# Expert rows of an AdaLN attention + MoE kernel: added onto the output in DRAM by indirect DMAs, in place of a buffer of picks, its loads and the last additions

## The reference

```python
# mod: six rows of 128 per batch from _silu(c) @ wmod; ga, gb with magnitude of at least 0.25
h = _layernorm(x) * (1 + ca) + sa
x = x + ga * attention(h)                      # "x1" below
h = _layernorm(x) * (1 + cb) + sb
x = x + gb * ffn(h)

def ffn(x):                                    # N = 4096 tokens, E = 8, K = 2
    topv, topi = top_k(x @ Wr + br, K); gates = softmax(topv)
    cap = N * K // E                           # 1024
    buf[e, rank] = token                       # rank < cap, others dropped
    h = gelu(x[buf] @ W1[e] + b1[e])
    out = h @ W2[e] + b2[e]
    final = zeros.at[buf].add(out * gate)      # scatter-add
    return final
```

## Time and profile before

| what | us |
|---|---|
| time, median of 3 runs (lowest, highest) | 561.09 (558.45, 562.75) |
| the profiled execution's own time | 562.52 |
| its span (first to last instruction of the program) | 560.8 |
| busy: TensorE (PE), DVE, POOL, ACT | 492.3, 374.6, 308.5, 280.7 |
| DMA: packets, MB, mean GB/s | 70928, 83.48, 149 |

### The profile page before, as it was taken

One profiled execution on the slowest core, in us unless ns is written; L12 is line 12 of the kernel. 1 busy time (PEld: TensorE's weight loads), 2 busy tenths in 40 slices (PEclk: granted clock), 3 DMA queues, 4 the chain that ended last, 5 costly groups with the idle time before them and its releaser, 6 DMA issues.

```text
span 560.8 us, 11087 instructions
## 1 busy us (share of the span) xinstructions
PE 492.3 (88%) x3550; PEld 271.4 (48%) x3566; DVE 374.6 (67%) x1303; ACT 280.7 (50%) x527; POOL 308.5 (55%) x558
## 2 busy tenths in 40 slices
PE   8699898999999999999999998984995799999830
PEld 4233353455455445545545544432483477777630
DVE  3489887789999999999999996240352033333353
ACT  1400685676776776676776767572340243332200
POOL 4330454465487678688677776463217544545650
PEclk9979998999999999999999999986998799999965
DMA  3578877546644754753643504113615154643059
GB/s 87 169 217 215 286 221 210 164 165 190 163 164 125 221 163 153 202 181 85 165 134 79 138 11 117 52 45 117 206 57 160 60 171 141 190 139 108 7 182 298
DMA packets 70928, 83.48 MB, mean 149 GB/s; under 512 B 8330, under 2 KB 59303, under 8 KB 68438
## 3 DMA queue, kind: packets, MB, share of 16 engines
q1 hardware_dynamic: 54582, 61.69, 38.6%
q10 hardware_dynamic: 11168, 13.05, 7.1%
q0 software_dynamic: 5120, 8.04, 4.4%
HBM read 44.79 MB, written 35.80 MB: 144 GB/s over the span
## 4 chain that ended last, share of the span: by engine, by line
PE 50%; DVE 19%; issue 16%; DMA 5%; another core or an unknown queue 2%; POOL 2%; ACT 2%; SPq 1%; DVEq 1%; ACTq 0%; POOLq 0%
PE ps L613 9%; PE ps L663 8%; PE ps L758 8%; PE ps L738 8%; DVE ps L1125 7%; PE ps L636 7%; DMA qrows<-mT 2%; PE ps L538 2%; DVE negmax L1125 2%; PE ps L576 1%; DVE negmax L1129 1%; DMA krows<-k_dram 1%; PE ps L619 1%; PE ps L581 1%
## 5 line engine op out<-in xcount | busy, mean ns | idle before, releaser
L915 ACT ACTIVATE prob<-ps 128x512 f32<-128x512 f32 (+1 forms) x352 | 182.8, 559 | 88.7 <-PE ps L636 66.6
L1125 DVE CUSTOM_DVE_ANT_0 ps<-ps,maskrow 128x512 f32<-128x512 f32 (+1 forms) x256 | 155.9, 639 | 17.8 <-PE ps L613 16.5
L1546 POOL TENSOR_SCALAR_AFFINE_SELECT prob<-prob 128x128 f32<-128x128 f32 (+2 forms) x308 | 104.0, 348 | 75.1 <-ACT prob L915 69.9
L613 PE MATMUL ps<-krows,qrows 72*128 72x128 bf16 (+3 forms) x512 | 131.1, 307 | 11.0 <-DMA krows<-k_dram 3.9
L636 PE MATMUL ps<-qrows,krows 75*128 75x128 bf16 (+3 forms) x512 | 127.9, 303 | 4.5 <-DMA qrows<-mT 2.5
L1594 POOL DMA_INDIRECT picks_dram<-qrows,dest x64 | 62.7, 979 | 52.4 <-DVE qrows L1353 35.5
L663 PE MATMUL ps<-prob,vpad 128*32 128x128 f32 (+3 forms) x1024 | 88.9, 454 | 1.2 <-ACT oS L922 0.7
L613 PEld LDWEIGHTS ps<-krows,qrows 72*128 72x128 bf16 x512 | 45.5, 99 | 89.5 <-DVE negmax L1125 43.9
L969 ACT ACTIVATE qrows<-ps,b_sb 128x512 f32<-128x512 f32 x64 | 41.0, 688 | 91.4 <-PE ps L738 66.9
L1583 POOL DMA_INDIRECT slots_dram<-rows,index x64 | 64.9, 1013 | 26.5 <-issue 15.2
L738 PE MATMUL ps<-qrows,vpad 128*128 128x512 f32 x128 | 60.7, 616 | 9.1 <-ACT qrows L969 9.1
(11 more groups left out here) (141 smaller groups left out, 542.8 us busy)
## 6 DMA issues: line engine op xcount, KB each, us to landing
qrows<-q_dram SPq DMA_DIRECT2D x48, 192.0 KB
krows<-k_dram SPq DMA_DIRECT2D x48, 192.0 KB
slots_dram<-empty ACTq DMA_DIRECT2D x32, 258.0 KB, 3.7
prob<-slots_dram SPq DMA_DIRECT2D x16, 516.0 KB
vpad<-in_w SPq DMA_DIRECT2D x30, 256.0 KB
k_dram<-kpart SPq DMA_DIRECT2D x40, 128.0 KB, 1.9
rows<-modB SPq DMA_DIRECT2D x8, 512.0 KB
picks_dram<-zeros ACTq DMA_DIRECT2D x8, 512.0 KB
```

The costliest lines, as they stand in the source:

```text
L613: last = mm(bank[:, i * w:(i + 1) * w], qrows[0:SROWS, b % 2, h, qb * P:(qb + 1) * P], krows[0:SROWS, b % 2, h, 0:w], start=(i == 0), stop ...
L915: fn(prob[:, s % PRING, 0:w], ps[:, TB + ring(s, TRING), 0:w], ACT.Exp, scale=SCALE)\
L1125: nc.vector.tensor_tensor_reduce(ps[:, SB_ + ring(s, SRING), 0:w], ps[:, SB_ + ring(s, SRING), 0:w], maskrow[:, T - w:T], -1.0, -NEG, ALU. ...
L1546: sel_(out=blk, in_=blk, compare_op=ALU.is_ge, fill=0.0, base=0, pattern=[[0, nh], [1, P]], channel_multiplier=-1).then_inc(S["masked"], 1)
```

## The change

There is no `picks` any more. x1 is stored to the output during attention, and every tile's rows are added onto the output in DRAM by the indirect DMA itself (`compute_op=ALU.add`), by the token's own number. Two experts may hold the same token, so a tile's sends wait until those of the two tiles before have landed, where these belong to another expert. Tile 15 (expert 7, upper half) does not wait for tile 14 (expert 7, lower half), since no token is in both.

Gone with `picks`: the zeroing (8 DMAs), the swap (8 small DVE instructions; the two instructions a batch that write the destinations become one copy), 16 loads, 16 DVE additions. The store of x1 stands on SP behind `copy_row`. The output rows stand in the order of tokens, so `tokid` counts partitions instead of blocks of four.

```diff
-FILL_AT = [UB + 44 + 3 * i for i in range(FILLS)] + [UB + 154 + 13 * i for i in range(ZEROS)]
+FILL_AT = [UB + 44 + 3 * i for i in range(FILLS)]
...
-        picks = nc.dram_tensor("picks_dram", [2 * N, C], F32).ap()
+        result = out.rearrange("b t c -> (b t) c")
...
+            def store_x1(b):
+
+                sp.wait_ge(S["x1_done"], b + 1)
+                sp.dma_start(out[b].rearrange("(j p) c -> p j c", p=P), xall[:, b]).then_inc(S["x1_out"], 16)
...
                     copy_row(b)
+                    store_x1(b)
...
-            pv = picks.rearrange("(k b p j) c -> b k p j c", k=2, b=B, p=P)
-            for k, tiles in ((0, 2 * E - 2), (1, 2 * E)):
-                for z in range(4):
-                    sp.wait_ge(S[f"picked{z}"], 16 * NT * ((tiles + 3 - z) // 4))
-                for b in range(B):
-                    sp.dma_start(two[:, b, k], pv[b, k]).then_inc(two_in[b // 2] if k else low_in[b // 4], 16)
-            for b in range(B):
-                sp.wait_ge(S["x2"], b + 1)
-                sp.dma_start(out[b].rearrange("(j p) c -> p j c", p=P), xall[:, b]).then_inc(S["out_done"], 16)
-            sp.wait_ge(S["out_done"], 16 * B)
+            sp.wait_ge(S["x1_out"], 16 * B)
+            for z in range(4):
+                sp.wait_ge(S[f"picked{z}"], 16 * NT * ((2 * E + 3 - z) // 4))
...
-                if s == R_SWAP:
-
-                    dve.wait_ge(S["r_best2"], b + 1)
-                    if earlier(b):
-                        dve.wait_ge(S["id_set"], 2 * b)
-                    tt(swap[:, :], best[:, 1, :], best[:, 0, :], ALU.is_gt).then_inc(S["r_swap"], 1)
...
-                    for k in range(2):
-                        stt(rows[:, u, k, :, DEST], swap[:, :], float(N - 2 * N * k), tokid[:, k, :],
-                            ALU.mult, ALU.add).then_inc(S["id_set"], 1)
+                    cp(rows[:, u, :, :, DEST], tokid[:, None, :].to_broadcast([P, 2, NT])).then_inc(S["id_set"], 1)
...
-            for k in range(2):
-                for b in range(B):
-                    add(b, k)
...
-            ms(zeros[:, :], 0.0).then_inc(S["consts"], 1)
...
-            nc.gpsimd.iota(tokid[:, :, :], [[N, 2], [1, NT]], base=0, channel_multiplier=NT,
+            nc.gpsimd.iota(tokid[:, :], [[P, NT]], base=0, channel_multiplier=1,
...
             def send(n):
 
                 if not earlier(n):
-                    pool.wait_ge(S["zeroed"], 16 * ZEROS)
+                    pool.wait_ge(S["x1_out"], 16 * B)
                 pool.wait_ge(S["dest_done"], n + 1)
+                for back in (1, 2):
+                    if earlier(n, back) and TILES[n - back][0] != TILES[n][0]:
+                        pool.wait_ge(S[f"picked{(n - back) % 4}"], 16 * NT * ((n - back) // 4 + 1))
                 for j in range(NT):
                     pool.wait_ge(S["y_done"], NT * n + j + 1)
-                    pool.indirect_dma_start(picks, bass.IndirectOffsetOnAxis(dest[:, n % 8, j:j + 1], 0),
-                                            yout[:, n % 4, j, :], None, bounds_check=2 * N - 1,
-                                            oob_is_err=False).then_inc(S[f"picked{n % 4}"], 16)
+                    pool.indirect_dma_start(result, bass.IndirectOffsetOnAxis(dest[:, n % 8, j:j + 1], 0),
+                                            yout[:, n % 4, j, :], None, bounds_check=N - 1, oob_is_err=False,
+                                            compute_op=ALU.add).then_inc(S[f"picked{n % 4}"], 16)
```

More of the change, by code:

```diff
@@ L291, in adaln_moe_kernel @@
         best = sb("best", [P, 2, NT])
-        swap = sb("swap", [P, NT])
         hot = sb("hot", [P, 2, NT, E])
@@ L314, in adaln_moe_kernel @@
         yout = qf[:, 5632:5632 + 4 * T].rearrange("p (a j c) -> p a j c", a=4, j=NT)
-        two = kf.rearrange("p (b k j c) -> p b k j c", b=B, k=2, j=NT)
         slotin = prob[:, :, :].rearrange("p a t -> p (a t)")[:, 0:SLOTS * NT * ROW]\
@@ L337, in adaln_moe_kernel @@
         w_in0 w_in1 w_in2 w_in3 slot_in0 slot_in1 slot_in2 slot_in3 slot_in4 slot_tr slot_T hid_mm hid_done y_mm y_add y_done dest_done
-        picked0 picked1 picked2 picked3 gb_in0 gb_in1 x2_low x2 out_done""".split()
+        picked0 picked1 picked2 picked3 gb_in0 gb_in1 x1_out""".split()
         S = {n: sem(n) for n in names}
-        two_in = [sem(f"two_in{b}") for b in range(0, B, 2)]
-        low_in = [sem(f"low_in{b}") for b in range(0, B, 4)]
         block = ctx.enter_context(nc.Block())
@@ L549, in _ @@
             pe.wait_ge(S["mod_T"], 4)
-            pe.wait_ge(S["consts"], 7)
+            pe.wait_ge(S["consts"], 6)
             pe.wait_ge(S["wqkv_in"], 48)
@@ L948, in prefill @@
                 if n == 0:
-                    act.wait_ge(S["consts"], 7)
-                if n < FILLS:
-                    z = slice(n * (E * CAP // P // FILLS), (n + 1) * (E * CAP // P // FILLS))
-                    act.dma_start(slots.rearrange("(p n) c -> p n c", p=P)[:, z, :],
-                                  empty[:, None, :].to_broadcast([P, E * CAP // P // FILLS, ROW]))\
-                        .then_inc(S["prefilled"], 16)
-                else:
-                    z = slice((n - FILLS) * (2 * N // P // 4 // ZEROS), (n - FILLS + 1) * (2 * N // P // 4 // ZEROS))
-                    act.dma_start(picks.rearrange("(p n m) c -> p n (m c)", p=P, m=T // C)[:, z, :],
-                                  zeros[:, None, :].to_broadcast([P, 2 * N // P // 4 // ZEROS, T]))\
-                        .then_inc(S["zeroed"], 16)
+                    act.wait_ge(S["consts"], 6)
+                z = slice(n * (E * CAP // P // FILLS), (n + 1) * (E * CAP // P // FILLS))
+                act.dma_start(slots.rearrange("(p n) c -> p n c", p=P)[:, z, :],
+                              empty[:, None, :].to_broadcast([P, E * CAP // P // FILLS, ROW]))\
+                    .then_inc(S["prefilled"], 16)
             def gelu(n):
@@ L1055, in modulation_columns @@
                 dve.wait_ge(S["mod_T"], 5)
-                dve.wait_ge(S["consts"], 8)
+                dve.wait_ge(S["consts"], 7)
             def modulation_rows():
@@ L1368, in finish @@
                     gated(n, j)
-            def add(b, k):
-                if k:
-                    dve.wait_ge(two_in[b // 2], 32)
-                    dve.wait_ge(S["x2_low"], b + 1)
-                elif b % 4 == 0:
-                    dve.wait_ge(low_in[b // 4], 16 * 4)
-                tt(xall[:, b], xall[:, b], two[:, b, k], ALU.add).then_inc(S["x2" if k else "x2_low"], 1)
             def step(n):
@@ L1566, in next_ids @@
             def next_ids(b):
-                pool.wait_ge(S["id_set"], 2 * (b + 1))
-                ts(tokid[:, :, :], tokid[:, :, :], float(T), None, ALU.add).then_inc(S["id_next"], 1)
+                pool.wait_ge(S["id_set"], b + 1)
+                ts(tokid[:, :], tokid[:, :], float(T), None, ALU.add).then_inc(S["id_next"], 1)
             def scatter(b, n):
```

18 lines of the change are left out of this document (7 added, 11 removed).

## The result

| | before | after |
|---|---|---|
| median of the runs, us | 559.77 (558.21 to 562.75, 4 runs) | 588.19 (585.34 to 591.66, 4 runs) |
| ratio to before | | 1.050, 95% interval 1.043 to 1.058 |
| profiled execution, us | 562.52 | 588.28 |
| its span, us; mean granted clock | 560.8; 0.942 | 586.6; 0.915 |

The changed kernel is 5% slower. I had said 547.3 and, in all, 0.63 for faster: both the time and the sign are wrong, and the time lies above the range as well. Rival 1, the sends as the bound, is what happened. In some executions of a kernel the time is longer at a lower granted clock; the ratios here leave these out, the medians do not.

A forecast was written before the change was run, and what follows sets the result against it. TensorE was busy 88%, but the last 18.7 us were the last send and its tail. Removing 15.0 and 0.3, against sends waiting 6.84 + 0.6 a tile, gave a span 13.8 shorter: 547.3 us, range 543 to 574.

The forecast's parts named there:

- Rival 1: At POOL's wait for send n-1: the sends become the bound, time 538.9 + 12x above x about 0.9; chance 0.43.
- POOL's time I leave, because nothing in the rows changed it but DVE: POOL's sends in the expert part: adding leaves each at 0.97 us and 1.28 apart, nothing added.
- x: Sends of the expert part: what adding costs over writing, a tile; taken as 0.6 us, bounded by 0 and 4.0.
- The landing's share: From POOL's end to the landing: an add lands 0.6 us later, 0.2 for moving bytes and 0.4 for a read.
- The cycle's skeleton: A tile's sends, start to start: 3.84 to the fourth, 0.97 its time, 1.26 landing, 0.77 restart; 6.84 us plus x.
- The threshold: Chain of sends: the time is even with before at x = 1.85, a cycle of 8.7 us.
- the formula of rival 1: Last send's landing when every tile from tile 3 on lags, from about x = 0.9: 538.2 + 12x.
- The end: Behind the last send's landing: SP has only its wait, so the span ends 0.4 us later.
- Rival 3: In attention: the stores of x1 delay the next batch, 5.4 us, giving 552.7; chance 0.04.
- Rival 2: In the last tiles: no lag, x under 0.3, and SP's k = 0 loads may cause a 3.00 us hold-up; 543 to 545, chance 0.13.
- The saving itself: At the end: loads, additions and stores behind the last landing go whole, 15.0 us saved.
- extra 0.3: Last send on POOL: 1.28 us beside DVE's additions against a median of 0.97, so 0.3 us goes with them.

The follow-up runs named there:

- the first experiment: The kernel before, with its 64 indirect DMAs to the buffer of picks adding instead of writing, no waits between tiles: 568.43 us, ratio 1.010.

## Why the prediction was wrong

**The step that failed** is "POOL's time I leave, because nothing in the rows changed it but DVE". It was kept out of x, and even its upper end (1.28, taken from a plain send's longest row) lay under what came: 1.55. x, taken as 0.6, measured 9.74 - 6.84 = 2.9: 1.74 from three longer pitches and 0.58 from the fourth send, together 2.3 of GpSimd's time, and 0.5 to 0.6 of later landing. The landing's share, 0.6 in the forecast, came out in size, but by luck: I made 0.2 of it from the moving of bytes, and it is as long for a tile with almost none. What the landing of an add waits for longer is open.

**The cycle's skeleton** (three pitches, the fourth send, the landing, the restart) was right where the landing is on time: 6.84 by the sum, 6.98 in the run that waits and writes. The threshold that I drew from it, even with before at x = 1.85 and a cycle of 8.7, left out the terms that follow. They add 13 us at x = 2.9, as much as 1.1 of x.

**With x = 2.9 the formula of rival 1 gives** a landing at 538.2 + 12 x 2.9 = 573.0, and it came at 582.6. The 9.6 between are: tile 3 at 456.50 in place of 451.76, 4.7 (the formula took tile 3's start from before, where it waited for DVE's rows of 450.58, while here DVE wrote them at 441.61 and tiles 0 to 3 already stood in the chain); tile 15, four longer pitches behind tile 14 (7.41 for 5.12), 2.3; and 2.7 for steps longer than 9.74 in tiles 3 to 14, above all the one behind tile 3, whose data landed late (469.51 in place of 466.2).

**The end** was "0.4 behind the last landing"; it is 3.9, since GpSimd's drain had been there in the trace before (542.6 + 7.46) and I did not ask what the removed tail was hiding besides the landing. 3.9 less 0.4 is 3.5. The sum closes: forecast 548.7 beside the profiled execution, + 26.4 (landing 546.6 to 573.0) + 9.6 + 3.5 = 588.2; measured 588.28.

**The rivals.** Rival 1 had the place, the formula and "POOL to take 0.3 longer an instruction" as its condition; it took 0.58 longer. I gave x beyond 2.3 a chance of 0.26 and let the range end at x = 2.9 without these other terms. Rival 3: TensorE waited for the maxima twice, 2.3 us in all, as before; wrong. Rival 2 suspected the loads behind the hole in the last tile. The chain of the run that writes without waiting, which has no loads there, shows such a hole too:

```profile
533.67 3.60 another core or an unknown queue
```

So the loads are not needed for it; what makes it stays open. The runs with adds or waits alone do not have it. The saving itself (15.0 us of loads, additions and stores gone) came about, as the forms that write show (14 and 17 us below before), but in the changed kernel the chain took it back and more.

**The two rules weighed.** The Trainium skill, "Collectives: The Full Stack", section "The bandwidth ceiling: the fold count and why AG ≠ RS ≠ AR", says of a ring's ReduceScatter that the add itself costs nothing and the second source read doubles the read side. The page has it from large collectives, and the measurement does not bear it out for these sends of 512-byte rows: 0.70 us of engine time for 64 KB where a write takes 0.20, more than a doubled read would give, and a GpSimd time 0.58 us longer an instruction, of which the rule says nothing. By the Trainium skill, "SBUF — State Buffer", section "Who interferes with whom", the last send should have lost its extra 0.3 with DVE's additions, and it did: it takes 0.97 in both forms that write and end without additions, and 1.55, the adding send's usual time, in the changed kernel. Where additions stayed, in the first experiment, a send beside them took longer again:

```profile
541.04 1.94 POOL L1594 DMA_INDIRECT picks_dram<-qrows,dest  x1 [0.30 <-issue]
```

The same section of the Trainium skill counts `tensor_tensor`, which these additions are, among what did not stall a DMA in its probe; these rows differ from that.

Not settled: what GpSimd does in the added 0.58 us (the runs show it as mostly a price per DMA), why single steps took 3 us and more beside SP's loads, and what held DVE's rows back in the kernel before.

## What to carry to other kernels

An instruction of a kind that the trace does not hold has no price in it: bound its time on the issuing engine as generously as its landing, and let the sum run at that end too before choosing a sign, above all where it is multiplied (64 times here) and stands in a chain with a wait. Ordering many small DMAs by their landings costs each group the whole of issue, landing and restart; it is nearly free as long as that sum stays about at what the other engines need for the same group (7.5 in the mean beside 7.4 to 7.7), and what lies above is paid in full (about 2.3 us in each of the 14 waits). Before a change is called cheap, see which engine was last in both kernels: here a hold-up in the kernel before covers part of what adding alone would cost. When a tail is cut off, read everything that ended inside it, each engine's drain too, since one of these is the new end.

## What the runs showed of the hardware that I had not expected

- An indirect DMA that adds keeps GpSimd for 1.55 us, a plain one of the same 128 rows for 0.97; for 64 rows 1.40 and 0.91. Both have 0.30 between one and the next.
- Adding takes 3.5 times the DMA engines' time of writing (0.70 against 0.20 us for 64 KB over 16 engines), in 144 packets a send against 32. It lands some 0.5 us later, and that hangs not on the bytes (2.61 us from GpSimd's end to the next start behind 0.26 MB and behind 0.04 MB). A DMA that adds 2 MB of DRAM onto DRAM took 12.8 and 13.2 us.
- GpSimd's drain at the end of the program ended 5.5 us after its last work where that was an adding send or a memset, 5.9 behind a plain send, and 14.8 and 15.1 behind the issue of a DMA of 2 MB, 3.0 after its landing.
- The kernel before took 534 us on one chip and 560 to 565 on the others; the chain of sends took 152 to 154 us on either.
